# Edge-count adjacency kernel: 128-row transfers, six-tile key windows with accumulated counts, H in three parts with a column of ones

## The reference, cut to what matters

```python
n1 = layernorm(x)                                   # 625 x 1024
u = n1 @ root + rbias
for r in range(8):                                  # relations
    mask = edge_type == r
    sums = segment_sum(n1[src] * mask, dst)         # 625 x 1024
    cnt  = segment_sum(mask, dst)                   # 625
    u += (sums / max(cnt, 1)) @ weight[r]
z = concat(u, n1) @ w_gate + gbias
x = x + tanh(u) * z + n1 * (1 - z)
x = x + int8_ffn(layernorm(x))                      # one scale for the whole tensor
x = x + gcn(layernorm(x))                           # out = D^-1/2 A D^-1/2 (h W + b)
x = x + top2_moe(layernorm(x))                      # 8 experts, capacity 196, + shared
```

## Time and profile before

| | us |
|---|---|
| time, median of 3 executions (lowest, highest) | 1477.52 (1457.95, 1479.84) |
| span of the profiled execution | 1453.2 |
| PE busy | 1152.1 (79%) |
| DVE busy | 765.1 (53%) |
| POOL busy | 432.5 (30%) |
| ACT busy | 388.9 (27%) |
| DMA | 200.76 MB, mean 138 GB/s |

### The profile page before, as it was taken

One profiled execution on the slowest core, in us unless ns is written; L12 is line 12 of the kernel. 1 busy time (PEld: TensorE's weight loads), 2 busy tenths in 40 slices (PEclk: granted clock), 3 DMA queues, 4 the chain that ended last, 5 costly groups with the idle time before them and its releaser, 6 DMA issues.

```text
span 1453.2 us, 13715 instructions
## 1 busy us (share of the span) xinstructions
PE 1152.1 (79%) x5203; PEld 906.0 (62%) x5203; DVE 765.1 (53%) x1230; ACT 388.9 (27%) x647; POOL 432.5 (30%) x284
## 2 busy tenths in 40 slices
PE   2659999999999999629466677756982899778993
PEld 1447777777777777517345455544861687657872
DVE  2429767867776412112345445443628747646644
ACT  1112232232223223011222222211414333315751
POOL 1005554445464555600111111110054501230023
PEclk8779999999999999859678888867995999979996
DMA  8554476765554444222322222234360210177855
GB/s 313 207 190 132 129 188 190 220 173 174 162 127 144 139 97 134 22 97 96 119 98 103 105 102 100 112 134 146 100 187 0 72 58 30 41 202 253 291 177 159
DMA packets 82465, 200.76 MB, mean 138 GB/s; under 512 B 33658, under 2 KB 34271, under 8 KB 73694
## 3 DMA queue, kind: packets, MB, share of 16 engines
q1 hardware_dynamic: 27444, 131.49, 26.1%
q0 software_dynamic: 35040, 21.99, 9.5%
q10 hardware_dynamic: 19908, 46.30, 9.0%
HBM read 141.21 MB, written 58.52 MB: 137 GB/s over the span
## 4 chain that ended last, share of the span: by engine, by line
PE 36%; DMA 31%; DVE 14%; POOL 8%; issue 5%; ACT 2%; ACTq 2%; SPq 1%; POOLq 0%; DVEq 0%
PE ps L481 30%; DMA stage<-h_scratch 8%; DMA adj_scratch<-cnt,idx 5%; POOL adj_scratch L1754 5%; DVE rl L334 5%; DMA AT<-adj_scratch 4%; DMA acb<-adj_scratch 3%; DMA stage<-in_w_e 3%; DMA stage<-in_w_gate 2%; DMA X<-in_x 2%; ACTq L948 1%; DVE U L1301 1%; DMA xn_scratch<-U 1%; ACT rh L326 1%; PE ps L743 1%
## 5 line engine op out<-in xcount | busy, mean ns | idle before, releaser
L334 DVE TENSOR_TENSOR rl<-stage,rh 128x512 fp32r<-128x512 f32 (+1 forms) x330 | 255.6, 805 | 488.4 <-ACT rh L326 488.3
L481 PE MATMUL ps<-rh,xTh 128*125 128x512 f32 x880 | 353.9, 402 | 75.3 <-DVE He L1273 39.6
L326 ACT CAST rh<-stage 128x512 fp32r<-128x512 f32 (+1 forms) x344 | 203.1, 622 | 646.6 <-PE ps L481 241.8
L481 PE MATMUL ps<-rl,xTh 128*125 128x512 f32 x880 | 351.7, 400 | 0.0
L481 PE MATMUL ps<-rh,xTl 128*125 128x512 f32 x880 | 349.8, 398 | 0.0
L1754 POOL DMA_INDIRECT adj_scratch<-cnt,idx x164 | 266.9, 1628 | 276.7 <-DMA adj_scratch<-cnt,idx 122.9
L481 PE MATMUL ps<-rh,Ar 125*125 125x512 f32 x400 | 173.9, 435 | 110.7 <-DVE rc L1291 96.0
L481 PEld LDWEIGHTS ps<-rh,xTh 128*125 128x125 f32 x880 | 165.9, 188 | 119.9 <-DVE He L1273 40.0
L481 PEld LDWEIGHTS ps<-rh,xTl 128*125 128x125 f32 x880 | 165.8, 188 | 43.0
L481 PEld LDWEIGHTS ps<-rl,xTh 128*125 128x125 f32 x880 | 165.8, 188 | 40.5
L481 PE MATMUL ps<-rl,Ar 125*125 125x512 f32 x400 | 170.0, 425 | 2.3 <-issue 2.3
(11 more groups left out here) (265 smaller groups left out, 1260.2 us busy)
## 6 DMA issues: line engine op xcount, KB each, us to landing
stage<-in_w_rel SPq DMA_DIRECT2D x32, 1024.0 KB
h_scratch<-He ACTq DMA_DIRECT2D x80, 250.0 KB
stage<-in_w_e SPq DMA_DIRECT2D x16, 1024.0 KB
adj_scratch<-Z ACTq DMA_DIRECT2D x16, 763.5 KB, 13.3
stage<-h_scratch SPq DMA_DIRECT2D x16, 750.0 KB
KR<-key_scratch ACTq DMA_DIRECT2D x41, 256.0 KB, 5.3
stage<-in_w_gate SPq DMA_DIRECT2D x8, 1024.0 KB
stage<-h_scratch SPq DMA_DIRECT2D x16, 500.0 KB
```

What stands on the lines that cost most here:

```text
L326: e.copy(h, s).then_inc(*a_hi.up(("hi", i)))
L334: e.tensor_tensor(l, s, h.bitcast(F32), ALU.subtract).then_inc(*own.up(("lo", i)))
L481: ins = e.matmul(ps[0:P, b, :], a, m, start=first and n == 0, stop=last and n == len(parts) - 1)
```

## The change

What it does, part by part:

- **128 rows.** Buffers in SBUF that were 125 partitions high become 128 high, with the name of the 125-row view kept; h, xn and zx scratch in DRAM get 128 rows. x chunks 0 to 3 are loaded as 128 rows (three of them belong to the next chunk), the last chunk as 112 + 13 rows. The adjacency is loaded as [128, 5, 625] with overlapping rows, H and ZX, XL as 128 rows, broadcasts to 128 partitions. `out` goes in 112 + 13 rows, 20 DMAs in place of 10. The edge lists lie in 112 rows of 128 in place of 82.
- **Queues.** Edge loads move from SP, behind the x loads, to the head of ACT's queue. The 16 zero fills move from ACT to POOL's queue, behind the five x chunks' arrival and ahead of the keys. n1 goes to xn_scratch by ACT, chunk by chunk, in place of one DMA of POOL. The memsets of the edge buffers move to POOL, which also zeroes He (128 x 4112) once.
- **Keys.** TG = 6, TILES = 162: 27 windows of six instructions of 128 x 768; each writes its count through accum_out, and the reduction is gone. WINDOWS = (1, 5), two in each half unit.
- **Adjacency.** A_0 and A_1 are loaded by POOL's queue right behind the last add (acb1 and Atot lie elsewhere, so that A_1 need not wait for He). A_r for r of 2 to 7 is loaded by SP behind the first part of H_(r-2), once A_(r-2) is cast. ACT casts A_1 ahead of the relations and A_(r+1) within relation r, one relation ahead.
- **Spread.** A row of H in DRAM is [1, 0, 1024 values]: HX = 1026 columns, in three parts of TH = 342, each one load (128 x 5 x 342), one cast, one subtraction and 50 matmuls, chunk by chunk (both results of a chunk's five tiles before the next chunk). Column 0 of part 0 is the count: per chunk DVE takes max(count, 1) and its reciprocal. The 80 ones-matmuls, crow and the 40 transposes are gone; PE has 1200 spread matmuls of 342 columns where it had 800 of 512.
- **SP's order behind the relations:** the last part of H_7, ZX twice, the first gate weights, XL, the other gate weights, x again in 128 rows.

The diff, cut to its core:

```diff
-TILES = 164
-TG = 4
+TILES = 162
+TG = 6
+HR = 112
-WINDOWS = (0, 2, 5)
+WINDOWS = (1, 5)
+HX = D + 2
+TH = HX // 3
+ROWS = [[(slice(0, 128), c * P, 128)] for c in range(C - 1)] + [[(slice(0, 112), 500, 112), (slice(112, P), 612, 13)]]
...
         for r in range(R):
-            for hf in range(2):
-                group(hd[r, hf][:, 0:1536], P, *[("h", r, hf, k) for k in range(3)])
-                group(hd[r, hf][:, 1536:2560], P, *[("h", r, hf, k) for k in range(3, 5)])
+            for q in range(3):
+                group(h_of(r)[:, :, q * TH:(q + 1) * TH], P, *[("h", r, q, k) for k in range(C)], width=TH)
...
-        adjacency = lambda r: accd[0:N * RI, :].rearrange("(c p f) o -> p c (f o)", c=C, p=P)[:, :, r * N:(r + 1) * N]
+        adjacency = lambda r: bass.AP(accd.tensor, r * N, [[RI, 128], [P * RI, C], [1, N]])
...
# SP
-            for i, a in enumerate((src, dst, typ)):
-                on.wait_ge(*at("er zero", i))
-                e.dma_start(er[i][:, 0, :], a[0:10496].rearrange("(p q) -> p q", q=128)).then_inc(*d_edge.up())
...
             def adjacency_in(r):
-                on.wait_ge(*at("added", TILES - 1))
-                if r >= 2:
-                    on.wait_ge(*at("adj", r - 2))
-                if r == 1:
-                    for unit in (R - 1, R):
-                        for hf in range(2):
-                            for c in range(C):
-                                on.wait_ge(*at("h_out", unit, hf, c))
+                on.wait_ge(*at("adj", r - 2))
                 e.dma_start(acr[r % 2], adjacency(r)).then_inc(*d_adj[r % 2].up(("acb", r)))
...
             for r in range(R):
-                for g in range(first("h", r, 0, 0), first("h", r, 0, 0) + 4):
-                    if g < first("gate", 0, 0) - 1:
-                        load(g)
-                if r + 1 < R:
-                    adjacency_in(r + 1)
+                for q in range(3):
+                    load(first("h", r, q, 0))
+                    if q == 0 and 2 <= r + 2 < R:
+                        adjacency_in(r + 2)
...
# PE
-                ins.then_inc(*product.up(("counts", r)))
...
-                by_tile(("spread", r, 0), tile["h", r, 0, 0], C, a_stat(r), freed(0), (("adj", r),))
...
+                for q in range(3):
+                    if (r, q) != (R - 1, 2):
+                        spread(r, q, nothing)
...
# ACT
-            for place in adj_zeros:
-                on.wait_ge(*at("Z"))
-                e.dma_start(place, Z[:]).then_inc(*d_zero.up(("adj zero",)))
             root("n1", 1)
+            xn_out(0)
...
# DVE
                     e.scalar_tensor_tensor(out=EQ[:, j, :], in0=KR[:, g % 4, :], scalar=kc[:, t:t + 1], in1=later[:, j0:j0 + TG * 128],
-                                           op0=ALU.is_equal, op1=ALU.mult).then_inc(*v_row.up(("equal", g)))
-                on.wait_ge(*at("equal", g))
-                e.tensor_reduce(cnt[:, cols], EQ[:], AX, ALU.add).then_inc(*v_row.up(("cnt", g)))
+                                           op0=ALU.is_equal, op1=ALU.mult, accum_out=cnt[:, t:t + 1]).then_inc(*v_row.up(("equal", g), ("cnt", g)))
...
+            def spread(r, q, c):
+                b, (cols, to) = banks.of["spread", r, q, c], PARTS[q]
+                on.wait_ge(*at("spread", r, q, c))
+                if q == 0:
+                    e.tensor_scalar(cn[:, r, c:c + 1], ps[0:P, b, 0:1], 1.0, None, ALU.max).then_inc(*v_out.up(("numbers", r, c)))
+                    on.wait_ge(*at("numbers", r, c))
+                    e.reciprocal(rc[:, r, c:c + 1], cn[:, r, c:c + 1]).then_inc(*v_row.up(("rc", r, c), ("rc", r)))
...
# POOL
+            for c in range(C):
+                on.wait_ge(*at("x", c))
+            for place in adj_zeros:
+                on.wait_ge(*at("Z"))
+                e.dma_start(place, Z[:]).then_inc(*d_zero.up(("adj zero",)))
...
+            for r in range(2):
+                on.wait_ge(*at("added", TILES - 1))
+                e.dma_start(acr[r], adjacency(r)).then_inc(*d_adj_first[r].up(("acb", r)))
```

More of the change, by code:

```diff
@@ L30 @@
 NS = 8 * CAP
-NSP = NS + 2 * N
+NSP = NS + 2 * C * 128
 NS7 = 7 * CAP
@@ L361, in load @@
             def load(g):
-                source, rows, n = groups[g]
+                source, width, n = groups[g]
                 name = next(k for k, i in tile.items() if tiles[i][0] == g)
@@ L376, in sync, with rows_in @@
+                e.dma_start(to, source).then_inc(*d_group[g % 2].up(("loaded", g)))
             first = lambda *name: tiles[tile[name]][0]
+            def rows_in(to, c, sem, *events):
+                for place, row, n in ROWS[c]:
+                    e.dma_start(to[place, c, :], x[row:row + n, :]).then_inc(*sem.up(*events))
             for c in range(C):
-                e.dma_start(U[:, c, :], x_v[:, c, :]).then_inc(*d_x[c].up(("x", c)))
+                if c == C - 1:
+                    on.wait_ge(*at("last rows zero"))
+                rows_in(U128, c, d_x[c], ("x", c))
@@ L480, in three @@
                 for n, (a, m) in enumerate(parts):
-                    ins = e.matmul(ps[0:P, b, :], a, m, start=first and n == 0, stop=last and n == len(parts) - 1)
+                    ins = e.matmul(ps[0:P, b, 0:width], a, m, start=first and n == 0, stop=last and n == len(parts) - 1)
                 return ins
@@ L1219, in vector @@
             e.memset(magt[:], MAGIC).then_inc(*v_row.up(("eps",)))
-            on.wait_ge(*at("ones"))
-            e.tensor_copy(ones2[:], onesf[0:P, 0:2]).then_inc(*v_row.up(("ones2",)))
-            on.wait_ge(*at("ident"))
-            e.tensor_copy(identb[:], ident[:]).then_inc(*v_row.up(("identb",)))
-            for i in range(3):
-                e.memset(er[i][:], 0).then_inc(*v_row.up(("er zero", i)))
+            e.memset(U128[96:128, C - 1, :], 0.0).then_inc(*v_row.up(("last rows zero",)))
             n1(0)
@@ new lines, in vector @@
+            for r in range(R):
+                for q in range(3):
+                    if (r, q) != (R - 1, 2):
+                        lows(tile["h", r, q, 0] + RT)
+                        for c in range(C):
+                            spread(r, q, c)
+                    if (r, q) == (R - 1, 0):
+                        e.tensor_reduce(sm[:, 5, :], cn.rearrange("p r c -> p c r"), AX, ALU.add).then_inc(*v_row.up(("counts summed",)))
+                        on.wait_ge(*at("counts summed"))
+                        e.tensor_reduce(qs[:, 4:5], sm[:, 5, :], AX, ALU.max).then_inc(*v_row.up(("most of each",)))
@@ L1723, in pool @@
             e.memset(onesf[:], 1.0).then_inc(*p_row.up(("ones",)))
-            e.memset(Z[:], 0.0).then_inc(*p_row.up(("Z",)))
+            for i in range(3):
+                e.memset(er[i][:], 0).then_inc(*p_row.up(("er zero", i)))
             on.wait_ge(*at("ones"))
```

318 lines of the change are left out of this document (153 added, 165 removed).

## The result

| | before | after |
|---|---|---|
| time, median us (lowest, highest) | 1469.35 (1457.95, 1479.84) | 1202.53 (1198.36, 1205.84) |
| span of the profiled execution | 1453.2 | 1204.1 |
| PE busy | 1152.1 (79%) | 1111.2 (92%) |
| DVE busy | 765.1 (53%) | 704.0 (58%) |
| DMA, mean GB/s | 138 | 168 |

The column before has one execution more than the table ahead of the prediction. The ratio is 0.8193 (95% interval 0.8141 to 0.8245).

A forecast was written before the change was run, and what follows sets the result against it. PE alone bounds the units; in the spreads it waits for the adjacency's rc and for He. Gains 24 + 40 + 138 + 22 + 7 = 231 off 1453.2 give span 1222, plus 16: 1238 us, range 1190 to 1300.

The forecast's parts named there:

- Start: Before the first unit: ACT freed of fills and a late edge load, units begin at 78 us, gain 24, bounds 5 to 32.
- Rival B: Start doesn't gain: fills on POOL's queue suffer while DVE norms and casts; 1262 to 1273 us, chance 0.17.
- Units: From unit (0,1) to the first spread: 19 half units of 28.0 us with PE never stalled, gain 40.
- Spreads: Spreads through transposes and flag: PE's waits go, by the load's engines first, look-ahead second; 216 us against 353.8, gain 138.
- POOL's hold on DVE: In the spreads: subtractions meeting POOL's sum take 8.69 us in place of 2.5, adding 6 us per relation.
- rival C: Spreads held by DVE without slack or slow H pieces, up to 32 us per relation: 1305 us, chance 0.14.
- Gates: Gates to the largest entry: x on 16 engines lands before the gates end, 65 us in place of 87.1, gain 22.
- Rest: End of the kernel: the last out, 11.9 us on the chain, goes faster in 112 rows; gain 7, bounds 0 to 8.
- From span to time: Added to the forecast span of 1222: 16 us, as measured times lay 4.7 to 26.6 above the one profiled span.
- D: Better than forecast: transposes and flag hide under the last loads, fills at full rate; 1200 to 1210 us, chance 0.07.
- A: The kernel runs as forecast: 1238 us, own range 1205 to 1262, chance 0.55.
- Rival E: Transfers don't spread: five engines still carry adjacency and H, 33 us of DMA per relation; above 1350 us, chance 0.03.

The follow-up runs named there:

- e4: The kernel before the change with only H and the adjacency written and loaded in 128 rows: 1330.1 us, ratio 0.9094 to before.
- e6: The changed kernel with the 16 zero fills moved back from POOL's queue to ACT's, behind the first casts: 1201.8 us, ratio 0.8180 to before.
- e8: The changed kernel with the fills placed behind the keys on POOL's queue: 1195.4 us, ratio 0.8139 to before.
- e9: The changed kernel with the first four key row loads put in ACT's queue at the first key window: 1188.6 us, ratio 0.8111 to before.
- e10: The changed kernel with the counts made by one reduction per window in place of accumulation: 1209.2 us, ratio 0.8249 to before.
- e3: The changed kernel with both H and the adjacency back in 125 rows: 1265.0 us, ratio 0.8641 to before.
- e5: The changed kernel with ZX, XL, x again and its accumulated n1 in 125 rows: 1246.1 us, ratio 0.8475 to before.
- e12: The changed kernel with out written in ten DMAs of 125 rows again: 1210.4 us, ratio 0.8260 to before.
- e1: The changed kernel with the loads of H alone back in 125 rows: 1236.8 us, ratio 0.8447 to before.
- e2: The changed kernel with the adjacency alone (loads, casts and sum) back in 125 rows: 1227.6 us, ratio 0.8391 to before.

## Why the prediction was right, and where it was off

**Bounds.** PE alone in the units, the adjacency and He behind it: right. e4 makes only the transfers of H and the adjacency faster and 133 us go.

**Start, 24 forecast, 26.8 measured.** The number was right, half of its reason wrong, and that is luck. I had ACT free of the fills as the gain; e6 gives them back and nothing changes, because 16 fills hold the keys on POOL's queue about as long as they held ACT. The keys land 20.6 us after their issue behind the fills, 2.6 ahead of them (e8) and 4.3 with the fills in another queue (e6). But e9 leaves the keys at 21.6 and is the fastest: what holds the units is ACT's queue, where the key rows stand ahead of casts that PE needs and of n1's last write. The forecast also slipped in its bounds: units from 67 us would be a gain of 35, not 32.

Rival B's mechanism fell. The fills went at share 1.00 and 403 GB/s while DVE was busy 5.56 of 8 us, and POOL's sixteen issues of them took 0.53 us in the median and 0.79 at most. The Trainium skill ("SBUF — State Buffer", "SBUF: two separate sides") warns that DVE in a two-port mode keeps POOL from writing descriptors. No loss of that kind shows here beyond the 0.26 us of the longest issue; which of these DVE instructions ran in such a mode the trace doesn't say.

**Units, 40 forecast, 40.2 measured.** 19 x 28.0 held to 0.1 us. The last add was issued at 526.3 and landed by 535.8, forecast 530; A_0 was wanted at 607, so 71 us of slack, forecast 80. A comparison took 1.017, forecast 1.03, and the count about nothing, as I took it. The rule in the Trainium skill, "Vector Engine (DVE) Microarchitecture Reference" ("7. Points that are easy to get wrong"), is for two sources that aren't bf16. Here one of two is bf16, and no half rate shows: 1.017 with the accumulation, 1.012 without (e10).

**Spreads, 138 forecast, 145.3 measured.** 342 columns took 0.157 (a part every 7.83 us, forecast 7.86). The stretch is 179.0 us for the parts (forecast 181) and 29.5 for the transposes, the flag and the last part (forecast 27). What never came is the friction of 8. The step that was mis-sized there is POOL's hold on DVE, 6 us per relation in my sum. The 24 subtractions take 54.6 us in all where 24 of the undisturbed 1.94 are 46.6, so it is 1 us per relation. DVE and POOL timelines at one such place:

```profile
733.12 3.72 DVE L349 TENSOR_TENSOR rl<-stage,rh 125x1710 fp32r<-125x1710 f32 x1 [0.77 <-ACT rh L339]
```
```profile
728.04 7.00 POOL L1770 TENSOR_TENSOR Atot<-Atot,Ar 128x3125 f32<-128x3125 f32 x1 [17.83 <-ACT Ar L935]
```

POOL's sum now begins while DVE adds from PSUM, which isn't held (0.57 us each beside the sum as without it), and the subtraction meets only its last 1.9 us. With that, DVE is busy 16.2 of 24 us and not 22 of 23.6, and rival C had no ground. The DMA share of 0.58 over 24 us is 14 us of transfers, between my 10 and 20. The forecast put the load's engines first and its place one relation ahead second. That order is not borne out: by e3 and e4 the engines and the other edits weigh the same, and the look-ahead by itself was never run.

**Gates, 22 forecast, 22.5 measured**, and e5 shows the cause as given: with 125 rows x is on the chain again.

**Rest, 7 forecast, 14.3 measured.** 9.2 of it lie behind the start of DVE's last additions, 15.0 us before and 5.8 after; e12 shows 5.2 of them to be the rows of out. The other 5 lie ahead: before, the chain's end held a gather of expert rows of 14.72 us (G<-eo_scratch,SI) that the chain after no longer has. These gathers land in 6.2 us in place of 13.9, and in e4 they still take 12.6, so it isn't the rows of H and the adjacency that made them faster. I had left the gathers out; the runs don't isolate the cause.

**From span to time, +16 forecast, -1.6 measured.** This is the largest miss, 17.6 us, and one of reading. In every run with both numbers the time is its own execution's span plus 1.7 to 2.2 us (1205.84 and 1204.1, 1265.19 and 1263.4). The profiled span of 1453.2 thus belongs to an execution of about 1455, a little under the fastest of all timed ones of before (1456.38 to 1487.97). The step that adds 16, because the times lay 4.7 to 26.6 above the span, carried the spread of the kernel before over to one that varies by 8 us only. Its adds, whose landings vary, stood on the path; after the change they have 71 us of slack. That this is why the spread went is argued, not shown: e4 keeps the adds on the path, and three of its four executions lie within 4.9 us of each other.

So the time of 1202.5 came out in D's place without D's reasons. The transposes and the flag didn't hide (29.5 us against 27), and only the fills ran at full rate, as D had it. Half of the 35.5 us between forecast and time is the reading of the span, the other half the small terms above. It lies in the stated range because that was wide. A's own range was narrower than its terms allow: added straight they give about 1203 to 1284, not 1205 to 1262.

Rival E's price per relation was about right (33 against 34 to 35), its total looks too high: if they add up, e3 and e5 together would be 1202.5 + 62 + 44, about 1309, not above 1350.

## What to carry to other kernels

Count the engines of every transfer before its bytes: here 128 rows in place of 125 for two tensors gave 133 us, and one transfer left on five engines cost 25 us although nobody waited for it, because it held the next one. Before saying which of two edits comes first, run each alone and leave each out: here either alone gave two thirds of the stage's gain. In an in-order queue, put a DMA that waits for a far event behind everything that the bound engine needs first. Each of e6 to e9 moved the same 20 us about, and only the one that passed all of PE's casts gave 14 back. Add a profiled span to the changes made on it, and take the offset to the measured time from single executions, not from the median of a kernel that varies.

## What the hardware showed that was not expected

- At a DMA share of 0.32 to 0.33, 125-row loads moved 126 GB/s in pieces of 2500 bytes and 118 GB/s in pieces of 1368 (e1): the piece hardly matters here, the share does.
- A transfer of 128 rows took 15 us in place of 6.3 with a 125-row transfer ahead of it (e2), and 16.7 in place of 10.1 with 125-row transfers beside it (e1).
- An accumulating comparison is two instructions in the trace, 1.017 and 0.085 us, but the next comparison starts 0.94 us after it, against 0.93 without accumulation (e10).
- POOL's sum holds DVE's subtraction only for what is left of it when the subtraction comes (3.72 in place of 1.94 us), so its price depends on the place and not on the two operations.
